# Convolution edge loop of a graph network: one TensorE signal for each step, and a new order inside the step

## What is computed

```
h = silu(edge_scalars @ W_fc1 / sqrt(10))          # 10 -> 100, per edge
w = h @ W_fc2 / sqrt(100)                          # 100 -> 128, per edge: w00, w11, w01, w10
x0e, x1e = y0[edge_src], y1[edge_src]              # gathered rows of the nodes
m00 = w00*x0e*sh0;  m11 = w11*sum(x1e*sh1)/sqrt(3);  m01 = w01*x0e*sh1;  m10 = w10*x1e*sh0
sums = segment_sum(concat(m00, m11, m01, m10), edge_dst)
```

## Time and profile before

| | us |
|---|---|
| median of three runs | 9544.22 |
| lowest, highest | 9513.62, 9572.33 |
| span of the profiled execution | 9589.4 |
| of it the convolution's edge loop, first to last L2014 start | 3558.9 to 6328.9 |

### The profile page before, as it was taken

How to read it: one execution, slowest core, us unless ns; L and a number is a source line. 1 busy time by engine, 2 the same in 40 slices (tenths; PEclk the granted TensorE clock), 3 DMA queues, 4 the chain that set the end, 5 groups by cost and what they waited for, 6 DMA issues and landing times. The chain is left out here.

```text
span 9589.4 us, 196015 instructions
## 1 busy us (share of the span) xinstructions
PE 7798.7 (81%) x51013; PEld 5815.8 (61%) x51014; DVE 6070.5 (63%) x12579; ACT 5243.3 (55%) x9302; POOL 3242.1 (34%) x3274
## 2 busy tenths in 40 slices
PE   5999999888699978888888777777777777777775
PEld 3656666677599966566556444445555555555554
DVE  7988998899844455555555455555555555555556
ACT  3666666788577754444444333345555555555553
POOL 0000000000000015555555556644555555454554
PEclk8999999999899988888888777788888888898897
DMA  3333333566466622222222111124555555454554
GB/s 114 138 132 137 139 136 138 190 225 223 149 183 183 183 85 58 57 57 58 56 58 57 43 43 44 44 70 144 149 147 151 152 148 148 143 159 144 149 157 124
DMA packets 627968, 1178.30 MB, mean 123 GB/s; under 512 B 215083, under 2 KB 288220, under 8 KB 608469
## 3 DMA queue, kind: packets, MB, share of 16 engines
q1 hardware_dynamic: 498618, 859.56, 28.2%
q0 software_dynamic: 129280, 317.93, 11.8%
HBM read 900.47 MB, written 276.57 MB: 123 GB/s over the span
## 5 line engine op out<-in xcount | busy, mean ns | idle before, releaser
L2250 POOL DMA_INDIRECT att_kv_rows<-kv_dram,att_stage x1616 | 1607.9, 995 | 1502.8 <-DVE att_msgs L2396 1013.5
L2005 POOL DMA_INDIRECT conv_rows<-y_dram,conv_stage x1616 | 1566.7, 969 | 1198.2 <-DVE conv_msgs L2077 678.1
L851 PE MATMUL att_mlp<-mlp_w,mlp_hid 128*128 128x128 f32 x6272 | 918.9, 296 | 397.8 <-issue 391.8
L851 PEld LDWEIGHTS att_mlp<-mlp_w,mlp_hid 128*128 128x128 f32 x6272 | 824.6, 206 | 471.7 <-issue 464.9
L1974 ACT ACTIVATE conv_hid<-conv_hid_ps 100x512 f32<-100x512 f32 x408 | 243.5, 597 | 1413.1 <-DMA y_dram<-mean_nodes_both 983.8
L695 PE MATMUL conv_part<-conv_msgs,conv_hot 128*128 128x256 f32 x3232 | 931.9, 437 | 50.1 <-issue 49.0
L2014 PE MATMUL conv_hid_ps<-conv_scalars,conv_w 10*100 10x512 f32 x816 | 529.1, 731 | 387.9 <-ACT conv_hid L1974 292.7
L695 PEld LDWEIGHTS conv_part<-conv_msgs,conv_hot 128*128 128x128 f32 x3232 | 690.5, 225 | 162.2 <-issue 64.0
L2223 ACT ACTIVATE acc<-att_q_ps 128x512 f32<-128x512 f32 x404 | 239.3, 592 | 985.9 <-DMA kv_dram<-conv_nodes_qkv 571.8
L842 PE MATMUL att_mlp<-mlp_feats,mlp_w 64*128 64x512 f32 x1568 | 558.4, 769 | 260.1 <-ACT mlp_hid L862 146.6
L235 PE MATMUL count_ps<-count_cols,count_rows 128*128 128x392 bf16 x3920 | 730.1, 331 | 8.6 <-DVE count_cols L201 8.6
(11 more groups left out here) (276 smaller groups left out, 15863.0 us busy)
## 6 DMA issues: line engine op xcount, KB each, us to landing
c_dram<-count_counts SPq DMA_DIRECT2D x392, 392.0 KB, 2.3
mean_counts<-c_dram SPq DMA_DIRECT2D x343, 448.0 KB, 3.4
w_dram<-mlp_w SPq DMA_DIRECT2D x404, 256.0 KB
att_w_rows<-w_dram SPq DMA_DIRECT2D x404, 256.0 KB
soft_counts<-c_dram SPq DMA_DIRECT2D x98, 1024.0 KB, 4.9
mlp_feats<-in_feats SPq DMA_DIRECT2D x405, 192.0 KB
soft_counts<-c_dram SPq DMA_DIRECT2D x49, 1088.0 KB, 5.0
att_lanes<-lo_dram SPq DMA_DIRECT2D x404, 128.0 KB
```

What stands on the lines that cost most here:

```text
L851: ins = nc.tensor.matmul(self.w_ps[:, t * D:(t + 1) * D], self.hid[:, n, t * P:(t + 1) * P], self.w1[:, n, :], start=n == 0, stop=n == 2 * ...
L2005: pool.indirect_dma_start(rows[:, s, t, :], None, y_dram, bass.IndirectOffsetOnAxis(ap=stage[:, s, t:t + 1], axis=0)).then_inc(gathered[s] ...
L2250: pool.indirect_dma_start(kv_rows[:, s, t, :], None, kv_dram, bass.IndirectOffsetOnAxis(ap=stage[:, s, t:t + 1], axis=0)).then_inc(gathere ...
```

## The change

In the convolution's loop PE signals once for each step, at the end of the scatter sums (`sums_done`), and all other engines wait for that one count. The order inside a step becomes `second`, `first`, the unit's quarter, scatter sums. ACT's silu of group g+4 waits for the end of step g (before: for `first` in step g). The message of group g waits for the end of step g-2 (before: for `second` in step g-2). ACT does the unit's two silus ahead of the one-hot rows. SP loads scalars and features behind `sums_done`. The products, their shapes and their number stay.

```diff
@@ tensor
-                pe.wait_ge(hid_done, g + 4)
-                first(s, i + 2)
-
-                pe.wait_ge(msg_done, 1 + g + 1)
-                second(g + 2, (s + 2) % S)
+                pe.wait_ge(msg_done, 1 + g + 1)
+                second(g + 2, (s + 2) % S)
+
+                pe.wait_ge(hid_done, g + 4)
+                first(s, i + 2)
+                if unit:
+                    mlp.tensor_quarter(nc, pe, U_CONV + i, s)
                 lane_sums(nc, pe, c, s, g, 2 * i + s // 2, msgs[:, s])
                 if s == 2:
                     turns(i, 1)
                 elif s == 0 and not early:
                     turns(i - 1, S - 1)
-                if unit:
-                    mlp.tensor_step(nc, pe, U_CONV + i, s, 1)
@@ first, second: no then_inc inside the loop; tensor_quarter: none either
@@ scalar
-                act.wait_ge(w_done, S * i + s + 1)
-                silu(S * (i + 1) + s, s)
+                act.wait_ge(c.sums_done, S + S * i + s + 1)
+                silu(s)
+                if unit and s < 2:
+                    mlp.scalar_quarter(nc, act, s)
                 if s < 2 or not last:
                     lane_hot(nc, act, c, (s + 2) % S, S * i + s + 2)
-                if unit:
-                    mlp.scalar_step(nc, act, U_CONV + i, s, 1)
@@ vector, message
-            dve.wait_ge(w_done, g + 1)
+            if first and s < 2:
+                dve.wait_ge(w_done, 1)
+            else:
+                dve.wait_ge(c.sums_done, S + g - 1)
@@ vector, body
                 if unit and s == 1 and not first:
-                    mlp.vector(nc, dve, U_CONV + i - 1)
+                    dve.wait_ge(c.sums_done, S + S * i)
+                    mlp.vector_of(nc, dve, U_CONV + i - 1)
@@ sync
-                        sp.wait_ge(hid_sum, S * i + s + 1)
+                        if first:
+                            sp.wait_ge(hid_sum, s + 1)
+                        else:
+                            sp.wait_ge(c.sums_done, S * i + s + 1)
                         load_scalars(s // 2, S * (i + 1) + s - 1)
                 if unit:
-                    mlp.sync_body(sp, U_CONV + i, 1, first)
+                    if not first:
+                        mlp.store(sp, U_CONV + i - 1)
+                    sp.wait_ge(c.sums_done, S + S * i + 2)
+                    mlp.load(sp, U_CONV + i + 1)
```

More of the change, by code:

```diff
@@ L869, in vector, with tensor_quarter, scalar_quarter, vector_of @@
                                 self.b1[:, 0].unsqueeze(1).to_broadcast([P, T, D]), ALU.add).then_inc(self.w_taken, 1)
+    def tensor_quarter(self, nc, pe, u, s):
+        if s < 2:
+            if s == 0:
+                pe.wait_ge(self.feats_in, 16 * (u + 1))
+            pe.wait_ge(self.hid_done, 2 * self.NC * u + 2 * s + 2)
+            for n in range(2):
+                half = slice(n * P // 2, (n + 1) * P // 2)
+                nc.tensor.matmul(self.hid_ps[:, n], self.w0[half, s * P:(s + 1) * P], self.feats[half, :], start=True, stop=True)
+        else:
+            if s == 2:
+                pe.wait_ge(self.hid_done, 2 + 2 * self.NC * (u + 1))
+                pe.wait_ge(self.w_taken, u + 1)
+            for t in range(T // 2 * (s - 2), T // 2 * (s - 1)):
+                for n in range(2 * self.NC):
+                    nc.tensor.matmul(self.w_ps[:, t * D:(t + 1) * D], self.hid[:, n, t * P:(t + 1) * P], self.w1[:, n, :],
+                                     start=n == 0, stop=n == 2 * self.NC - 1)
+    def scalar_quarter(self, nc, act, s):
+        for n in range(2):
+            nc.scalar.activation(self.hid[:, 2 * s + n], self.hid_ps[:, n], ACT.Silu, bias=self.b0[:, 2 * s + n:2 * s + n + 1]).then_inc(self.hid_done, 1)
+    def vector_of(self, nc, dve, u):
+        dve.wait_ge(self.w_stored, 16 * (u + 1))
+        nc.vector.tensor_tensor(self.w[:], self.w_ps.rearrange("p (t f) -> p t f", t=T),
+                                self.b1[:, 0].unsqueeze(1).to_broadcast([P, T, D]), ALU.add).then_inc(self.w_taken, 1)
+    def tensor_skip(self, pe, units):
+        pe.sem_inc(self.hid_sum, 2 * self.NC * units)
+        pe.sem_inc(self.w_sum, units)
     def tensor_step(self, nc, pe, u, s, per):
@@ L1971, in _, with silu @@
             def _(act):
-                def silu(g, s):
-                    act.wait_ge(hid_sum, g + 1)
+                def silu(s):
                     nc.scalar.activation(hid[:, s], hid_ps[0:100], ACT.Silu, scale=10 ** -0.5).then_inc(hid_done, 1)
@@ L1977, in body @@
                     for s in range(S):
-                        act.wait_ge(w_done, S * i + s + 1)
-                        silu(S * (i + 1) + s, s)
+                        act.wait_ge(c.sums_done, S + S * i + s + 1)
+                        silu(s)
+                        if unit and s < 2:
+                            mlp.scalar_quarter(nc, act, s)
                         if s < 2 or not last:
                             lane_hot(nc, act, c, (s + 2) % S, S * i + s + 2)
-                        if unit:
-                            mlp.scalar_step(nc, act, U_CONV + i, s, 1)
                 for g in range(S):
-                    silu(g, g)
+                    act.wait_ge(hid_sum, g + 1)
+                    silu(g)
                 for g in range(2):
@@ L2013, in first @@
                     n = s % 2
-                    nc.tensor.matmul(hid_ps[0:100], w1[rows_of(n)], scalars[rows_of(n), s // 2, :], start=True, stop=True).then_inc(hid_sum, 1)
+                    return nc.tensor.matmul(hid_ps[0:100], w1[rows_of(n)], scalars[rows_of(n), s // 2, :], start=True, stop=True)
                 def second(g, s):
@@ L2019, in second @@
                         ins = nc.tensor.matmul(w_ps[:, s % 2, t, :], hid[:, s, t * P:(t + 1) * P], w2[:], start=True, stop=True)
-                    ins.then_inc(w_done, 1)
+                    return ins
                 tensor_lane_start(pe, c)
@@ L2025, in _ @@
                         pe.wait_ge(hid_done, s)
-                    first(s, 1)
+                    first(s, 1).then_inc(hid_sum, 1)
                 second(0, 0)
-                second(1, 1)
+                second(1, 1).then_inc(w_done, 1)
                 def turns(i, s):
@@ L2051, in _ @@
                     body(i, False, True)
+                mlp.tensor_skip(pe, N_CONV)
                 with pe.Fori(N_CONV, NI) as i:
@@ L2057, in _, with message @@
             def _(dve):
-                def message(i, s):
+                def message(i, s, first):
                     g = S * i + s
@@ L2091, in body @@
                     for s in range(S):
-                        message(i, s)
+                        message(i, s, first)
                         if s == 1 and not first:
```

4 lines of the change are left out of this document (3 added, 1 removed).

## The result

| | us |
|---|---|
| before, median of four runs (lowest, highest) | 9537.56 (9513.62, 9572.33) |
| changed, median of four runs (lowest, highest) | 9624.41 (9613.64, 9626.69) |
| ratio, 95% interval | 1.0085 (1.0058 to 1.0112) |
| span of the profiled execution, before and changed | 9589.4 and 9611.7 |

In a second batch the changed kernel stood at 9628.11 beside 9548.47, a ratio of 1.008 (1.0059 to 1.010). So it is slower, by 80 to 87 us, where 194 were forecast.

A forecast was written before the change was run, and what follows sets the result against it. The loop was taken as bound by runs of gathers and stops for held PE signals. Longer circles, +72 us without units and +122 with, sum to +194 on 9544: 9738 us, range 9400 to 9920.

The forecast's parts named there:

- What bounds the loop: Convolution loop: gathers run until held PE signals stop POOL; 2.2 us to signal arrival plus 2.07 to restart, 4.23 standing.
- the rival without holds: Loop paced by gathers (5.05 us a step) or PE (5.3 with units) if signals are rarely held; 8897 us, chance 0.22.
- When a signal passes: PE's signals beside gathers: they stick between 20 and 26 MATMUL records after a run of gathers begins.
- The walk: Step-by-step timing of PE and POOL after a held signal arrives; gave +72 us without units and +122 with units.
- The number of signals: Rival: the count of PE signals is what sticks, so one a step rarely does; 647 us less, 8897 us, chance 0.22.
- The silu behind the scatter sums costs nothing: ACT's silu, 0.60 us, is hidden by `second`, 0.99 us, with prompt signals; uncovered it would cost 242 us.
- More stops: POOL's stops for a free row buffer: 150 to 190 with units (134 before), about 75 without (60 before).
- the walk with units: Timing of unit iterations after a release: 8.15 or 7.1 us a step, half and half 7.5 against 7.0, +122 us.
- The length of a stop: POOL at a hold: signal arrives 2.2 us behind the last gather, gathers restart about 2.1 us after that.
- the walk without units: Timing of unit-free iterations: two steps in 14.5 us or three in 19.5, mean 6.95 against 6.5, +72 us.
- the circle: Convolution loop: a run of gathers, 2.2 us until held signals arrive, 2.07 us until gathers restart.
- the circle stays as long as it is: Rival: runs keep 1.8 and 2.7 steps, only terms near 0 remain; 9544 us, or 9515, chance 0.21.

The follow-up runs named there:

- half_records: Changed kernel with two of four tiles in second-layer product and scatter sums after the first steps, eight fewer MATMUL records a step: 9549.98 us beside 9562.32 before.
- half_columns: Changed kernel with half the columns in second-layer product and scatter sums, all MATMUL records kept: 9664.69 us beside 9562.32 before.
- before_again: Unchanged copy of the kernel before, profiled on a chip that holds signals: 9533.02 us beside 9562.32 for before itself.

## Why the prediction was right in its direction and wrong in its size

**What bounds the loop: right.** Signals of PE held beside the gathers. The forecast had it from the timeline alone; the plain loads took 871 us off the same chip's time, some 664 of them for the holds, and a chip without held signals ran the loop at the two rates that the rival without holds was given. That chips exist which hold nothing was in no reading of the forecast.

**When a signal passes: right.** Between 20 and 26 records; half_records and half_columns confirm records against time and columns (14 and 22 passed, 24 and 26 held). The walk did not know that a stop of about 1 us leaves the count running, but it had no stop so short.

**The number of signals (rival, 0.22): out.** 9 signals a step against 1 are 0.2%.

**The silu behind the scatter sums costs nothing: right, as placed.** PE's busy time per step did not change. What the cover is worth was undersized: 379 us, on a chip that does not hold, not 242.

**More stops: right.** 150 to 190 with units were forecast and 184 came; about 75 without, and 90 came. In stops per step: the walk with units has 4 in 5 steps, 0.80, measured 184 / 240 = 0.77; without units 3 in 7, 0.43, measured 90 / 160 = 0.56. Runs of 4 and 8 gathers with units came (105 and 48 of 178; stops of under 1 us are not counted here as ends), and without units 8 was forecast and it is 4 and 8 by turns (48 and 39 of 105). Twelve had stood there before only without units (38 of 62 runs); with units it was eight (84 of 134). The walk missed the fours there because it freed the buffer 1.3 us behind the signal, and by the timeline it is 2.2 to POOL's restart (5852.91 to 5855.09), the same 2.07 to 2.2 that it uses at a hold.

**The length of a stop: this step failed.** "Gathers restart at 2.1", "held, arriving at 12.3 + 2.2": the sum took 2.2 us from the last gather to the signal, read behind a run of twelve, for runs of four and eight. But the release came sooner in the changed kernel: behind the 8 gathers of the walk without units it is 1.3 in the median, behind 4 it is 0.9; and where the signal was never held but only late, as at 5852.91, the stop is 1.5 us. All of POOL's pauses of over 0.6 us in the changed kernel, parted by whether the signal had been held, say it in the walk's terms. With units the walk has stops of 4.3 behind a hold and of 2.1 behind a late signal; measured are 2.8 (116 stops) and 2.3 (91). Without units it has 4.3 throughout; measured are 3.0 behind a hold (61) and 1.8 behind a late signal (52), a kind that the walk without units did not have. In the kernel before the stops behind a hold are 4.4 us long in both stretches. In the walk's own form, a step is 5.05 us of gathers and its share of stops. With units: forecast 5.05 + 0.80 x 3.1 = 7.5, measured 5.05 + 0.77 x 2.74 = 7.16 (the windows say 7.08). Without (where (29 + 19.5)/7 is 6.93 and not the 6.95 of the forecast, 3 us on the sum): forecast 5.05 + 0.43 x 4.4 = 6.9, measured 5.05 + 0.56 x 2.66 = 6.54 (6.52). Against the 6.97 and 6.50 of before that is +0.11 to +0.19 a step instead of +0.5, and +0.02 to +0.04 instead of +0.45. The profiled executions scatter by as much: one on another chip that holds, before_again, has 985 gathers in 1700 us, 6.90 a step, against which the change is +0.18 x 244 = 44 us with units; its whole span, 9531.2, is 80 below that of the changed kernel.

**So** the circle got more turns and shorter ones. Each hold in the walk was counted at the stop's old length, where the stop's length changed with the kernel; why it did is only in part the length of the run. The rival "the circle stays as long as it is" (0.21) was wrong in its reason, the run lengths did change, but with 9544 it was nearer to 9624 than the forecast with 9738. The measured time is inside the range of 9400 to 9920; of the chances, the one for "within 1%" (0.23) held, not the 0.55 for slower by over 1%.

## What to carry to other kernels

When a loop is a circle with a stop in it, do not price the new circle with the old stop: part the stops of the trace by kind (held or only late) and by what stands before them, and forecast each kind for itself. Here the mean of 3.4 us with units against 3.8 without hid that the stops with the silu's signal held were 4.4 in both. It would not have given the whole answer: the kernel before has 1.8 us behind eight gathers, which would have brought the forecast only part of the way from 2.2 to 1.3. Before tuning waits around a signal that is late, find out what makes it late: here plain transfers in the place of the gathers were worth 9% on a chip that holds, 7% of it for the held signals, and the change 0.8%. And one signal at the end of a step was free, on a chip that does not hold, only with a product between it and its reader; with the order undone it cost 4.6%.

## What the runs showed of the hardware that I had not expected

- Two kinds of chips: the same kernel before takes 8062 to 8090 us in two batches and 9514 to 9620 us in all others. On the first no PE signal is late beside indirect gathers, on the second they are held by up to some 10 us from the 20th to 26th MATMUL record of a run of gathers on, and a stop of about 1 us does not start that count anew. Which chip has it, and why, is open.
- With plain transfers of the same size nothing is held on either, whether SP or GpSimd starts them (8731 and 8722 us). A plain start on GpSimd takes 537 ns of it, an indirect one 965 to 1017 (means of the profiles).
- The release comes 0.9 us behind the last gather of a run of four, 1.3 to 1.8 behind eight, 1.8 to 2.3 behind twelve, 2.8 behind sixteen.
- Sparing records lets the runs grow and with them the stops: half the products of the second layer and the sums, and a step without units still takes 6.45 us.
- With half the records or half the columns in two of the three product groups the granted clock was 0.50 and 0.51 from 5290 to 6200 us, where it was 0.79 in the changed kernel, though PE was busy 682, 753 and 692 of the 910 us. So leaving out products did not shorten PE's time.
